# A mixture-of-experts stage with split-float matmuls: the fifth pass of the gate and of the value weight on 64 rows each

## The reference, cut to what matters

```python
def _expert(xf, W1, W2, W3):
    gate = jnp.minimum(xf @ W1, LIMIT)
    up = jnp.clip(xf @ W3, -LIMIT, LIMIT)
    return jax.nn.silu(gate) * up @ W2
...
flat = x.reshape(-1, D)                       # (1128, 192)
scores = jnp.sqrt(jax.nn.softplus(flat @ gate_w))
_, indices = jax.lax.top_k(scores + gate_bias, K)    # 2 of 8 experts for each token
...
y = _expert(flat, w1s, w2s, w3s)              # the shared expert, for all tokens
h = jax.nn.silu(gate_h) * up_h                # gate_h, up_h: the routed experts, width 768
routed = jnp.einsum('etd,te->td', jnp.einsum('eti,eid->etd', h, w2), combine)
return (y + routed).reshape(B, T, D)
```

## Time and profile before

| | |
|---|---|
| median of 3 runs | 896.37 us (890.22 to 903.12) |
| profiled execution, time | 885.85 us |
| profiled execution, span of its instructions | 883.9 us |
| PE / PEld busy | 697.8 / 586.7 us (79% / 66%) |
| DVE, ACT, POOL busy | 494.8, 334.5, 248.9 us |
| mean granted TensorE clock | 0.874 of full |

### The profile page before, as it was taken

One profiled execution on the slowest core, in us unless ns is written; L12 is line 12 of the kernel. 1 busy time (PEld: TensorE's weight loads), 2 busy tenths in 40 slices (PEclk: granted clock), 3 DMA queues, 4 the chain that ended last, 5 costly groups with the idle time before them and its releaser, 6 DMA issues.

```text
span 883.9 us, 13338 instructions
## 1 busy us (share of the span) xinstructions
PE 697.8 (79%) x4972; PEld 586.7 (66%) x4972; DVE 494.8 (56%) x1253; ACT 334.5 (38%) x735; POOL 248.9 (28%) x257
## 2 busy tenths in 40 slices
PE   3249799999889942754188878787999999999994
PEld 3249656666866732211177767577899899999994
DVE  2277846534410169666226566744665877777771
ACT  0034601431433112452154554440523566666551
POOL 3542422221000000002523222323046044444432
PEclk9769958999789985556588999998899999999998
DMA  8900300001000050003900000010033767777743
GB/s 207 197 18 3 108 1 1 1 1 49 6 1 0 1 137 2 1 0 84 265 5 1 5 3 4 5 56 17 2 134 119 278 198 215 217 227 227 228 117 62
DMA packets 36618, 70.80 MB, mean 80 GB/s; under 512 B 6877, under 2 KB 27576, under 8 KB 34218
## 3 DMA queue, kind: packets, MB, share of 16 engines
q0 software_dynamic: 12128, 45.63, 17.9%
q1 hardware_dynamic: 24426, 24.32, 10.1%
HBM read 59.76 MB, written 10.67 MB: 80 GB/s over the span
## 4 chain that ended last, share of the span: by engine, by line
PE 60%; DVE 13%; issue 11%; POOL 6%; DMA 6%; ACT 2%; SPq 1%; POOLq 0%; DVEq 0%; ACTq 0%
PE bank L1582 8%; PE bank L1301 4%; PE bank L1184 4%; PE bank L1552 2%; PE bank L1549 2%; PE bank L1553 2%; PE bank L1551 2%; PE bank L1550 2%; PE bank L1274 2%; PE bank L1311 2%; POOL x_slots L775 2%; PE bank L1227 2%; PE bank L1224 2%; DVE big L1730 2%; PE bank L1421 2%
## 5 line engine op out<-in xcount | busy, mean ns | idle before, releaser
L2099 DVE TENSOR_SCALAR big<-bank 128x256 f32<-128x256 f32 (+1 forms) x126 | 52.0, 413 | 52.1 <-PE bank L1553 51.8
L728 POOL TENSOR_TENSOR big<-big,arc 128x423 f32<-128x423 f32 (+1 forms) x48 | 38.1, 816 | 100.2 <-DVE arc L2062 100.2
L1084 ACT ACTIVATE big<-bank 128x256 f32<-128x256 f32 (+1 forms) x126 | 47.7, 379 | 44.8 <-PE bank L1553 44.8
L2042 DVE TENSOR_REDUCE amx<-bank 128x3 f32<-128x423 f32 (+1 forms) x48 | 26.0, 542 | 67.5 <-PE bank L1421 52.9
L761 POOL DMA_INDIRECT total<-big,goal x32 | 54.1, 1690 | 23.3 <-ACT big L1074 14.4
L1549 PE MATMUL bank<-x_lead,w_lead 128*128 128x256 f32 x192 | 56.4, 294 | 0.0
L1552 PE MATMUL bank<-x_both,w_lead 128*128 128x256 f32 x192 | 54.5, 284 | 0.0
L1553 PE MATMUL bank<-x_both,w_rest 128*128 128x256 f32 x192 | 54.2, 282 | 0.0
L1551 PE MATMUL bank<-x_lead,w_rest 128*128 128x256 f32 x192 | 54.1, 282 | 0.0
L1550 PE MATMUL bank<-x_rest,w_lead 128*128 128x256 f32 x192 | 53.9, 281 | 0.0
L2110 DVE SCALAR_TENSOR_TENSOR big<-big 128x256 f32<-128x256 f32 (+1 forms) x126 | 49.9, 408 | 0.1
(11 more groups left out here) (498 smaller groups left out, 1978.4 us busy)
## 6 DMA issues: line engine op xcount, KB each, us to landing
x_slots<-creg SPq DMA_DIRECT2D x2, 1552.0 KB, 17.9
big<-x_slots SPq DMA_DIRECT2D x16, 194.0 KB, 4.8
big<-in_patches SPq DMA_DIRECT2D x1, 1536.0 KB, 8.2
areg<-in_e_gate_up SPq DMA_DIRECT2D x1, 1536.0 KB, 24.7
shared_lead<-in_e_gate_up POOLq DMA_DIRECT2D x1, 1536.0 KB, 7.0
wreg<-in_ffn_w SPq DMA_DIRECT2D x1, 1152.0 KB
out<-total SPq DMA_DIRECT2D x2, 423.0 KB
wreg<-in_in_w SPq DMA_DIRECT2D x2, 419.0 KB
```

What stands on the lines that cost most here:

```text
L1084: nc.scalar.activation(GS[:, n % 3, 0:w], bank[2 * (n % 2)][:, 0:w], ACT.Silu).then_inc(S["g_silu"], 1)
L2099: v.tensor_scalar(UM[:, n % 3, 0:w], bank[2 * (n % 2) + 1][:, 0:w], 10.0, -10.0, ALU.min, ALU.max).then_inc(S["u_clip"], 1)
```

## The change

In every step, shared and routed, the two fifth passes now use 64 rows each. The gate's takes rows 0 to 63 of the weights' rests and of `x_both` (the tokens' leads). The value's takes rows 64 to 127 of the weights' rests, and so needs the tokens' leads in rows 64 to 127: a new tile `x_twin` (`XT`) holds them, written by one more ACT copy in each `lead_x`. The value's fifth pass comes first in its group, directly behind the gate's, so that the two stand next to each other. The product rest x rest of the last 64 inner rows is no longer computed. DVE's wait in `rest_x` counts three copies instead of two.

```diff
+        XT = [lead_rest(f"x_twin{k}", big1_at, 9 * SLOTS + 2 * TT * XW + 4 + k * SLOTS, SLOTS, F32R) for k in range(2)]
...
                 nc.scalar.copy(XB[g % 2][0:DB, 0:w], b).then_inc(S["x_lead"], 1)
+                nc.scalar.copy(XT[g % 2][DB:P, 0:w], b).then_inc(S["x_lead"], 1)
...
+                tail = [XB[g % 2][0:DB, 0:w], XT[g % 2][DB:P, 0:w]]
...
-                    for q in range(2):
-                        o = bank[2 * (n % 2) + q][:, 0:w]
-                        a, b = slice(q * P, (q + 1) * P), slice((2 + q) * P, (3 + q) * P)
-                        mm(o, wh[:, a], xh, start=True, stop=False)
-                        mm(o, wh[:, a], xr, start=False, stop=False)
-                        mm(o, wl[:, a], xh, start=False, stop=False)
-                        mm(o, wh[:, b], xb, start=False, stop=False)
-                        mm(o, wl[:, b], xb, start=False, stop=True).then_inc(S["gu_mm"], 1)
+                    gate, value = (bank[2 * (n % 2) + q][:, 0:w] for q in range(2))
+                    mm(gate, wh[:, 0:P], xh, start=True, stop=False)
+                    mm(gate, wh[:, 0:P], xr, start=False, stop=False)
+                    mm(gate, wl[:, 0:P], xh, start=False, stop=False)
+                    mm(gate, wh[:, 2 * P:3 * P], xb, start=False, stop=False)
+                    mm(gate, wl[0:DB, 2 * P:3 * P], tail[0], start=False, stop=True).then_inc(S["gu_mm"], 1)
+                    mm(value, wl[DB:P, 3 * P:4 * P], tail[1], start=True, stop=False)
+                    mm(value, wh[:, P:2 * P], xh, start=False, stop=False)
+                    mm(value, wh[:, P:2 * P], xr, start=False, stop=False)
+                    mm(value, wl[:, P:2 * P], xh, start=False, stop=False)
+                    mm(value, wh[:, 3 * P:4 * P], xb, start=False, stop=True).then_inc(S["gu_mm"], 1)
...
-                dve.wait_ge(S["x_lead"], 2 * (g + 1))
+                dve.wait_ge(S["x_lead"], 3 * (g + 1))
```

More of the change, by code:

```diff
@@ L113, in build @@
         prod = sb("prod", [P, TT])
+        big1_at = -(-nc.sbuf_base // 32) * 32
         big1 = sb("big1", [P, KH * TP])
```

## The result

The changed kernel takes 935.12 us in the median of four runs (931.70 to 941.32) against 895.52 for the kernel before on the same chip: 4.4% slower, ratio 1.044 with an interval of 1.035 to 1.054. That is 39.6 us more. The profiled execution is the slowest of the four, with a span of 939.5 us.

What follows compares the result with a forecast made beforehand. PE's own work was taken to bound the routed items. Routed +27.8, wait -1.7, shared items 2 to 4 +3.9 and 0 and 1 +2 gave +32 us on 896.37, so 928 us, range 917 to 941.

Steps and rivals of the forecast that it cites:

- the wait of 1.7 us: Routed items: PE's 1.71 us wait for the slots' DMA goes, covered by the longer item in front, -1.7 us.
- PE sets the end in the routed items, one to one: Routed items: whatever PE does more or less goes into the time; 96 steps x 0.29 = +27.8 us.
- A pair runs side by side and saves 0.12: Each step: two matmuls on different row halves start within 0.01 us, saving one slot of 0.12 us.
- The way in and out: Each step: switching to 64 rows and back drains PE; 0.77 us where 0.48 was, +0.29 us a step.
- The copy, the wait on DVE and the order cost nothing: Token leads and fifth passes: 21 more ACT copies, rest_x 0.27 us later, value's fifth pass in front; +0 us.
- Shared items, +5.9: Shared items: +3.9 us in items 2 to 4 and +2 us in items 0 and 1, switches less waits.
- two steps at the lower of its two levels: First shared items: clock not yet full for two steps, PE's work taking twice as long, 2 x 0.29 = 0.6 us.
- The clock falls: Routed stretch: PE stands still more, clock granted 0.9 instead of 1.00, some 20 us more, 948 us; chance 0.05.
- No switch cost: Each step: pair goes in and out without a wait, saving 0.12 us; 883 us, 1.5% faster; chance 0.05.
- hidden loads: Each switch: one 0.11 us load hides under the fourth pass, 0.07 a step, +7 to +9, 904 us; chance 0.06.
- Halves that don't overlap: Each step: the second half follows at 0.12, costing 0.11 us more, +14 in all, 942 us; chance 0.04.

Runs made afterwards that it cites:

- two_steps: Changed kernel with the half-row pairs of two steps put next to each other, one way in and out for two steps; 1.0075 of the kernel before.
- gate_half: Kernel before with only the gate's fifth pass on rows 0 to 63, the value's on 128 rows, no copy or new order; 1.047 of the kernel before.
- apart: Changed kernel with the value's half-row matmul last in its group, so each half-row matmul stands alone between 128-row ones; 1.127 of the kernel before.
- full_rows: Changed kernel with both fifth passes on all 128 rows again, keeping the order, copy and longer DVE wait; 0.995 of the kernel before.
- again_b: Changed kernel without edits, measured and profiled a third time; 1.039 of the kernel before.
- shared_only: Changed kernel with the half-row pair in the 30 shared steps only, routed steps on 128 rows; 886.21 us against 878.03 for the kernel before, 1.010.
- again: Changed kernel without edits, measured and profiled a second time; 913.87 us against 879.05 for the kernel before, 1.034.
- rows96: Kernel before with both fifth passes on rows 0 to 95; 0.999 of the kernel before.

## Why the prediction was right

The time of 935.1 us lies in the stated range and on the side forecast; the sum was +32 us, and +39.6 was measured on the first chip, +34.8 and +33 on others. The 39.6 lies at the very end of what the terms themselves allowed (28 to 39, a time of 924 to 935 us, where the 39 leaves the wait of 1.7 us in place without saying so), so on that chip the number held with nothing to spare and leans on the margin for the scatter of the runs.

*PE sets the end in the routed items, one to one.* Right: the stretch grew by 23.9 us for 25.4 us of steps and 1.7 us of wait absorbed, the very wait that was named.

*A pair runs side by side and saves 0.12.* Right (800.66 and 800.66), and shown to be worth its 0.12 in `two_steps`.

*The way in and out.* Right in kind and nearly in size: 0.75 us where the prediction added up 0.77, so a step of +0.265 for +0.29. The excess of 0.02 is no more than rounding can give, with five rows of 0.01 us added up. `gate_half`, `two_steps` and `apart` each follow from the same price to 0.1 us an item.

*The copy, the wait on DVE and the order cost nothing.* Right (`full_rows`).

*Shared items, +5.9.* Right for the switches (+4.9 in again_b), too small on the whole: +7.0 in the profile of `shared_only` and +8.2 in its time, +13 and +26.5 in two profiles of the change. The step that was mis-sized is the 0.6 us for "two steps at the lower of its two levels". It took the rise of the clock as given and only asked what the switches cost while it was low. For a single step even that was too much (a step at the lower level takes 2.51 us against 2.13, so 0.38 more and not 0.58), but the low time itself was longer in some executions: 3.5 us for the late rise in `again`, and 4.6 for the fall in the fifth item, in it and in the first profile. The stop of ACT, DVE and PE makes up most of that profile's +26.5 (some 17 us, when the 4.9 of the switches and the 4.6 of the fall are taken off), and its cause stays open.

*The rivals.* "The clock falls", with a chance of 0.05, was placed in the routed items, where the clock is at 1.00 in each profile; it came true on a small scale in the fifth shared item, in some executions. No switch cost, and hidden loads, fall with the timeline of a step. Halves that don't overlap fall with 800.66. The Trainium skill's rule of the drain ("TensorEngine Tiling (Array Packing)", Key Properties) held in each run that changed between 128 and 64 rows, and so did its qualification, not just the tile: inside `two_steps`, where only the half changes, the second pair adds 0.12 us in all. `rows96` fits it too, since the list of tilings there (Tiling Modes) has 64 and 32 rows but none of 96. What that page promises under Theoretical Speedup for small matmuls, up to twice the speed for an inner dimension of 64, is true of the pair (both start at 800.66) and false of the step (1.465 us against 1.20).

## What to carry to other kernels

A half-row pair saves one slot, and the way in and out of 64-row matmuls costs the drain and the bare weight load twice (here 0.39 us beyond the slots, or some three slots); count pairs per switch before you count rows. Read PE by the distance from start to start: its busy share was 79% before and after, while a step had become 22% longer. And where a stage follows a slack stretch, look at the granted clock in small windows in more than one profile, before the change and after, and not only at the work under the full clock: two executions of the same changed kernel differ by some 8 us there.

## What was not expected of the hardware

The same kind of sparser stream kept the full clock in one place and lost it in another. In the routed items it was at 1.00 over 207 us with one way in and out in a step of 1.465 us, and over 253 us with two in 1.96 us. In the fifth shared item, with its 128-column matmuls (steps of 1.30 us in the changed kernel), it fell for 10 to 14 us in four of six profiles, without a wait of PE before it. After a slack stretch it took 3.0 to 5.9 us at the lower level to rise without half-row matmuls, 3.8 to 13.5 in five profiles with one way in and out per step, and 44 with two. Why one execution has the late rise or the fall and the next of the same kernel has not stays open. The same kernel's items repeat to 0.01 us (13.08 and 13.09 in a row), so that +0.1 us an item is plain in one profile, while the whole time scatters by 1%.
